# Attention heads handled four at a time instead of two at a time in a fused decoder kernel

## The reference, cut to what matters

```python
def local_attention(q, k, v):            # 16 heads of 64, windows of 64 tokens
    ...
    sim = jnp.einsum('bhwie,bhwje->bhwij', bq, bk2) * QK_SCALE
    sim = jnp.where(mask, -jnp.finfo(sim.dtype).max, sim)
    attn = jax.nn.softmax(sim, -1)
    out = jnp.einsum('bhwij,bhwje->bhwie', attn, bv2)
...
for i in range(DEPTH):                   # 6
    x = attn_layer(shift_tokens(x), Wqkv[i], q_scale[i], k_scale[i], Wo[i]) + x
    x = ffn_layer(shift_tokens(x), ln_g[i], ln_b[i], W1[i], b1[i], W2[i], b2[i]) + x
```

## Time and profile before

| | us |
|---|---|
| median of 3 runs | 3348.35 (3347.62 to 3349.45) |
| the profiled execution, its own time | 3347.67 |
| its span in the profile | 3345.9 |
| ahead of the first feed-forward block (first L831) | 260.7 |
| an ordinary slot | 62.4 |
| the longer slots at a change of layer | 67.0 to 76.4 |
| TensorE / VectorE / ScalarE / GpSimd busy | 2950.3 / 2440.5 / 2211.5 / 1464.3 |

### The profile page before, as it was taken

One profiled execution on the slowest core, in us unless ns is written; L12 is line 12 of the kernel. 1 busy time (PEld: TensorE's weight loads), 2 busy tenths in 40 slices (PEclk: granted clock), 3 DMA queues, 4 the chain that ended last, 5 costly groups with the idle time before them and its releaser, 6 DMA issues.

```text
span 3345.9 us, 83253 instructions
## 1 busy us (share of the span) xinstructions
PE 2950.3 (88%) x26408; PEld 2463.4 (74%) x26408; DVE 2440.5 (73%) x8851; ACT 2211.5 (66%) x6256; POOL 1464.3 (44%) x1052
## 2 busy tenths in 40 slices
PE   6778998888999888999988999988999988898996
PEld 5567877777777767777776777766777767777775
DVE  3477777777777777777777777777777777777773
ACT  3357667666676666767666766766676666667663
POOL 3354454334444444445443444433544543454450
PEclk9899999999999999999999999999999999999997
DMA  4210010111001111100112010012101011110000
GB/s 136 68 40 23 17 30 22 40 57 53 22 17 30 42 50 49 30 22 17 30 53 71 18 30 22 17 40 76 35 20 27 24 41 48 35 32 27 27 26 21
DMA packets 109664, 124.10 MB, mean 37 GB/s; under 512 B 11589, under 2 KB 84129, under 8 KB 109473
## 3 DMA queue, kind: packets, MB, share of 16 engines
q1 hardware_dynamic: 109472, 121.75, 12.7%
HBM read 73.50 MB, written 16.78 MB: 27 GB/s over the span
## 4 chain that ended last, share of the span: by engine, by line
PE 44%; DVE 27%; ACT 11%; issue 11%; DMA 2%; DVEq 1%; POOL 1%; SPq 0%; ACTq 0%; POOLq 0%
PE project L791 12%; PE wide L844 7%; DVE with_sin L1137 6%; PE acc L859 6%; PE score L878 5%; DVE sums_sq L1134 4%; PE acc L821 4%; DVE probs L1215 4%; DVE probs L1223 3%; PE turned L891 2%; PE mix L905 2%; DVE sums_sq L1139 2%; ACT L982 2%; ACT with_sin L949 2%; ACT probs L1019 2%
## 5 line engine op out<-in xcount | busy, mean ns | idle before, releaser
L791 PE MATMUL project<-w_qkv,xT 128*128 128x512 f32 x3456 | 953.3, 415 | 37.8 <-DVE xT L1117 33.8
L1050 POOL TENSOR_TENSOR query_scale<-sums_sq,half 128x8 f32<-128x8 f32 x192 | 412.9, 2151 | 1230.8 <-DVE sums_sq L1139 1225.8
L1019 ACT ACTIVATE probs<-probs,shift 128x128 f32<-128x128 f32 x1536 | 605.4, 396 | 430.5 <-DVE shift L1215 425.2
L791 PEld LDWEIGHTS project<-w_qkv,xT 128*128 128x128 f32 x3456 | 628.2, 194 | 172.7 <-DVE xT L1117 41.9
L1215 DVE CUSTOM_DVE_ANT_0 probs<-score,mask,query_scale 128x128 f32<-128x128 f32 x1536 | 468.7, 342 | 304.1 <-PE score L878 290.3
L844 PE MATMUL wide<-nT,w_up 128*128 128x256 f32 x3456 | 493.6, 293 | 149.2 <-ACT gates L982 87.5
L844 PEld LDWEIGHTS wide<-nT,w_up 128*128 128x128 f32 x3456 | 444.5, 194 | 201.9 <-ACT gates L982 108.9
L1053 POOL TENSOR_TENSOR inv_norm<-sums_sq,half 128x8 f32<-128x8 f32 x192 | 411.2, 2141 | 224.5 <-DVE sums_sq L1139 223.1
L1223 DVE TENSOR_SCALAR probs<-probs,inv_sums 128x128 f32<-128x128 f32 x1536 | 381.5, 291 | 0.0
L1134 DVE TENSOR_REDUCE sums_sq<-with_sin 128x8 f32<-128x512 f32 x384 | 261.8, 682 | 78.8 <-ACT with_cos L950 78.6
L1137 DVE TENSOR_TENSOR with_sin<-with_cos,tables 128x512 f32<-128x512 f32 x384 | 301.9, 786 | 13.3
(11 more groups left out here) (121 smaller groups left out, 5099.3 us busy)
## 6 DMA issues: line engine op xcount, KB each, us to landing
v_mid<-v SPq DMA_DIRECT2D x192, 128.0 KB, 2.3
staging<-in_w_qkv SPq DMA_DIRECT2D x24, 768.0 KB
y_in<-y_scratch SPq DMA_DIRECT2D x48, 256.0 KB, 2.8
res<-y_scratch SPq DMA_DIRECT2D x48, 256.0 KB, 2.7
y_scratch<-res SPq DMA_DIRECT2D x40, 256.0 KB, 2.4
staging<-in_w_up SPq DMA_DIRECT2D x12, 682.0 KB
staging<-in_w_out SPq DMA_DIRECT2D x6, 1024.0 KB
xn<-res SPq DMA_DIRECT2D x48, 112.0 KB, 2.3
```

The costliest lines, as they stand in the source:

```text
L791: last = pe.matmul(project[(x - 1) % 2][:], xT[a][:, h, t * P:(t + 1) * P], w_qkv[w][:, h, c, g, :], start=(h == 0 and (a, w) == PASSES[0] ...
L1019: last = act.activation(probs[:, t % 4, cols], probs[:, t % 4, cols], ACT.Exp, bias=shift[:, t % 2, i:i + 1], scale=-1.0, accum_out=sums[: ...
L1050: pool.tensor_tensor(query_scale[:, u // 2, g * GROUP_HEADS:(g + 1) * GROUP_HEADS], sums_sq[:, u, :], half[:, 0:GROUP_HEADS], ALU.pow).the ...
```

## The change

Heads are handled in quads. In tick 0 of every four TensorE scores four heads and mixes the quad before. VectorE masks two heads in tick 0 and two in tick 1, and scales two in tick 1 and two in tick 2; ScalarE's exponentials stand in ticks 0 and 1, ahead of its cast of `oT`. TensorE transposes two heads in tick 2 and two in tick 3. The casts of `oT` and their low parts cover four heads in one instruction, the latter one tick later; the reciprocals cover two heads. `probsT` holds four heads and `shift` four; `score` uses all of its 512 columns; `w_up` is laid out anew to make room. `SCHEDULE` is as it was. The core of the diff (names on the + side have other line numbers after the change):

```diff
-            def pair_scores(s, t, H):
+            def quad_scores(s, t, H):
...
-                for w, first in enumerate((0, 0, WINDOW, P)):
-                    for side, rows in enumerate(sides):
...
+                for k in range(QUAD_HEADS // 2):
+                    pair = t // 2 + k
+                    for w, first in enumerate((0, 0, WINDOW, P)):
+                        for side, rows in enumerate(sides):
+                            at = k * BAND + (w // 2) * P
+                            last = pe.matmul(score[side][sides[w % 2], at:at + P], qT[rows, pair, w * WINDOW:(w + 1) * WINDOW],
+                                             kT[rows, pair, first:first + P], start=True, stop=True)
+                            if w == 3:
+                                last.then_inc(scores_ready, 1)
+
+            def turn_pair(k, H):
+
+                pe.wait_ge(probs_scaled, H + 2)
+                wait(pe, probsT_copied, H)
...
-                    if t % 2 == 0 and s.head(t, 0) is not None:
-                        pair_scores(s, t, s.head(t, 0))
-                    if t % 2 == 0 and s.head(t, 4) is not None:
-                        pair_mix(s.n, (t - 4) % HEADS, s.head(t, 4), s.n * PAIRS + (t - 4) // 2)
-                    if t % 2 == 1 and s.head(t, 2) is not None:
-                        turn_pair((t - 2) % HEADS, s.head(t, 2))
+                    q = t % QUAD_HEADS
+                    if q == 0 and s.head(t, 0) is not None:
+                        quad_scores(s, t, s.head(t, 0))
+                    if q == 0 and s.head(t, 4) is not None:
+                        quad_mix(s.n, (t - 4) % HEADS, s.head(t, 4), s.n * PAIRS + (t - 4) // 2)
+                    if q == 2 and s.head(t, 2) is not None:
+                        turn_pair(0, s.head(t, 2))
+                    if q == 3 and s.head(t, 3) is not None:
+                        turn_pair(2, s.head(t, 3) + 2)
...
+                    q = t % QUAD_HEADS
+
+                    k = 2 * (q % 2)
+                    H = s.head(t, q)
+                    if H is not None and q < 2:
+                        for j in range(k, k + 2):
+                            act.wait_ge(scores_masked, H + j + 1)
+                            for i in range(TILES):
...
+                    if H is not None and q >= 2:
+                        act.wait_ge(probs_turned, H + k + 2)
+                        wait(act, mixed, H)
+                        act.copy(probsT[:, k:k + 2, :].rearrange("p a b -> p (a b)"), turned[:]).then_inc(probsT_copied, 2)
                     H = s.head(t, 4)
-                    if H is not None and t % 2 == 0:
+                    if H is not None and q == 0:
...
+                        act.copy(oT[0][:, pair:pair + 2, :], mix[:]).then_inc(out_high, 2)
...
+                    done = 2 * (q - 1)
+                    if H is not None and q in (1, 2):
+                        dve.wait_ge(exp_done, H + done + 2)
+                        dve.reciprocal(inv_sums[:, done:done + 2, :], sums[:, done:done + 2, :]).then_inc(sums_inverted, 2)
+                    if H is not None and q < 2:
...
+                        dve.wait_ge(scores_ready, H + QUAD_HEADS)
+                        wait(dve, probs_turned, H)
+                        for k in (2 * q, 2 * q + 1):
...
+                    if H is not None and q in (1, 2):
+
+                        dve.wait_ge(sums_inverted, H + done + 2)
+                        for k in (done, done + 1):
...
+                    if q == 1 and s.head(t, 5) is not None:
...
+                        dve.tensor_tensor(oT[1][:, pair:pair + 2, :], mix[:], oT[0][:, pair:pair + 2, :].bitcast(FP32),
+                                          ALU.subtract).then_inc(out_split, 2)
```

More of the change, by code:

```diff
@@ L570, in sem @@
             return ctx.enter_context(nc.semaphore(name))
-        w_qkv, w_out, w_up, w_down = W.qkv, W.out, W.up, W.down
+        w_qkv, w_out, w_up, w_down = W.qkv, W.out, W.up_flat, W.down
         params = sb("params", [P, 2 * FFN_TILES + 2 * HALVES])
@@ L862, in dense @@
                     last.then_inc(h_used, 1)
-            def pair_scores(s, t, H):
-                pair = t // 2
+            sides = [slice(HEAD_DIM * side, HEAD_DIM * side + HEAD_DIM) for side in range(2)]
+            def quad_scores(s, t, H):
                 if t % GROUP_HEADS == 0:
@@ L1213, in slot @@
-                        dve.sem_inc(passed, 1)
-                        for i, (a, b) in enumerate(((0, P), (P, BAND))):
-                            last = dve.tensor_tensor_reduce(out=probs[:, t % 4, a:b], in0=score[t % 2][:, a:b], in1=mask[:, a:b],
-                                                            scale=query_scale[:, i, t:t + 1], scalar=3e38, op0=ALU.add, op1=ALU.min,
-                                                            accum_out=shift[:, t % 2, i:i + 1])
-                        last.then_inc(scores_masked, 1)
```

95 lines of the change are left out of this document (37 added, 58 removed).

## The result

The changed kernel takes 3679.96 us (median of 4 runs, 3670.98 to 3718.72), against 3347.98 us before: a ratio of 1.102, with a 95% interval of 1.093 to 1.110. It is slower, as forecast, but by 332 us where 200 were forecast (3548), and it lies above the range of 3430 to 3640. The profiled execution is the longest of the four, 3718.72 us.

What follows compares the result with a forecast made beforehand. TensorE sets the pace but no engine is full, so list order decides its idle time. Stretches of 1.9 + 0.5 + 1.8 = 4.2 us per slot, in all 200 us, take 3347.7 to 3548; range 3430 to 3640.

Steps and rivals of the forecast that it cites:

- the clock: Rival: clock falls in ordinary slots too, two waits each costing 1.3 us more, 125 us, total 3670; chance 0.10.
- its own last part: Signs to look for: first gate's wait 2.4 us, second's 2.1, last `down` about 1, ordinary slots 66 to 67 at clock 1.00.
- The sum of the waits: Added TensorE waits over all slots: 4.2 us for each slot, half in the first, in all 200 us.
- scores of tick 8 to those of tick 12: Stretch around the gates: later `nT`, GELU and copy make it 1.8 to 1.9 us longer.
- ticks 12 to 15: Stretch up to the last `down`: VectorE's longer list in tick 13 delays it, net 0.5 us.
- ticks 0 to 8: Stretch with rotations and projections: later scales and other waits, less the lost wait for masks, net 1.8 us.
- First gate: Ticks 8 and 9, behind `nT`: starts 1.65 us later, at 6.9, of which 0.85 are wait.
- Second gate: Tick 9, behind ScalarE's GELU: 5.2 us behind the first gate instead of 4.44, 0.75 more; wait from 1.4 to about 2.1.
- Last `down`: TensorE's last `down`, behind VectorE's 2.6 us list in tick 13 and a 2.6 us chain: starts 1.0 us after TensorE is free.
- Transposes of tick 3: Transposes of the second pair's probabilities wait 1.9 us for VectorE's scales, which stand behind the later rotations.
- waits absorb one another: Rival: VectorE and ScalarE catch up while TensorE waits, half the sum stays, 100 us, total 3448; chance 0.12.
- Not slower: Rival: cover in TensorE's list suffices for all three chains, total 3300 or 3348; chance 0.07, of which 0.04 faster.

Runs made afterwards that it cites:

- Experiment 4: Kernel before the change, with one more head's exponentials on ScalarE ahead of the other work of ticks 8 and 9: 3460.72 us, ratio 1.034.
- experiment 1: Changed kernel with filler matmuls on TensorE ahead of the waits of the first gate, second gate and last `down`: 3553.46 us, ratio 1.062.
- experiment 2: Changed kernel with filler matmuls at one place only: ahead of the last `down` 3613.16 us; ahead of the two gates 3624.21 us.
- experiment 8: Kernel before with fillers at two gates: 3340.20 us; sized, in weight-loading slots only: 3332.61; those plus four ahead of tick 9's transposes: 3333.49.
- experiment 7: Changed kernel with token scaling and the cast of `nT` ahead of the exponentials in ScalarE's tick 8: 3694.84 us, ratio 1.105.
- experiment 5: Kernel of experiment 1, one filler instead of three ahead of the last `down`, VectorE's scaling of two heads omitted in ticks 1 and 13: 3486.01 us.
- experiment 6: Changed kernel with tick 3's transposes of the quad's second pair behind the first half of the output projection: 3700.15 us, ratio 1.106.

## Why the prediction was wrong, and where it was right

**The step that failed is the clock.** The forecast's sum has nothing for it, and says that ordinary slots keep a clock of 1.00; all 30 of them have a stretch at 1.2 GHz, and the clock costs 127 us. The text read the 2.91 us behind a wait of 2.22 us, priced the fall into ordinary slots at 125 us (measured: 127) and its case at 3670 (measured: 3680), and then gave it 0.10. What it set against it was that waits of 1.19 and 1.37 us leave the clock at 1.00. But by its own last part these waits become 2.4 and 2.1 us long, the length of the wait in the earlier trace rows and not of those in the earlier trace rows. The forecast checked its waits against the clock of the kernel before, not against that of its own kernel. Experiment 4 brackets the difference on the kernel before: with waits of 1.19 and 1.37 no ordinary slot has a fall, with 1.75 and 2.15 all but one of 30 have. That the price came out so near is in part luck. The text had two falls of 1.3 us in every slot. The profiled execution has two stretches in nearly every ordinary slot, of which some are free, some cost 1.5 us and some 3, on the mean 3.4 us for each of these slots, and 165 us over the profiled execution of experiment 1; the other three executions of the changed kernel are 31 to 48 us shorter. The Trainium skill, "TensorE: Matmul & The Clock Gate", Part 1, has the low level as the default that activity releases; experiments 1, 2 and 8 agree, as useless matmuls hold the clock.

**The sum of the waits was right,** 200 us forecast, 207 measured with the clock held (experiment 1), 4.2 against 4.7 for an ordinary slot. By the text's three stretches, on the mean of the ordinary slots of experiment 1 against those before: scores of tick 8 to those of tick 12, 1.9 forecast, 1.6 measured; ticks 12 to 15, 0.5 forecast, 1.2 measured; ticks 0 to 8, 1.8 forecast, 1.9 measured.

That the sum holds is partly luck too, because one gain was left out. The waits of an ordinary slot grow from 4.6 to 10.4 us where the second gate waits in full, 5.8 more, and the slot by only 4.7. The rest is TensorE's own: from the start of a quad's scores to the end of its mixes 2.09 us pass (1067.32 to 1069.41), where two pairs took twice 1.19 (1501.37 to the row below), and over four quads that is 1.2 us less. The text took 0.6 for a pair's scores and 0.6 for its mixes in either kernel.

```profile
1502.56 0.66 PE L831 MATMUL wide<-ident,xn 128*128 128x128 f32 x4
```

By terms:

- First gate: the sum had the wait grow by 0.85, which gives 2.04; the text's last part says 2.4; 2.55 measured. Its start, 1.65 later by the forecast, is 1.47 later. Shown in experiments 4 and 7 to be ScalarE's list.
- Second gate: 2.1 forecast, 2.14 where the clock held ahead of it. Shown in experiment 4.
- Transposes behind the third gate: 0.25 forecast, 0.19.
- Last `down`: 1.0 forecast, 1.76 measured. This is the one term that was clearly mis-sized. The length of VectorE's list (2.6 us forecast, 1095.54 to 1098.08 measured) and of the chain behind it (2.6 forecast, 2.5 measured) were right, and experiment 5 confirms that the list sets the wait. The list begins too early in the forecast. With the `down` 0.5 us later than before and 5.2 us of list and chain ahead of it, the list would start about 5.6 us behind the scores of tick 12 (an estimate from the text's numbers); it starts 6.5 behind them. What holds it there follows below.
- Transposes of tick 3: 1.9 forecast, 1.69 measured. The mechanism was named half: experiment 6 shows a second chain, over GpSimd, that is as late, so the late start of the rotation is the cause, and not the place of the scales.
- The fourth projection 0.35 and tick 6 0.35: 0.41 and 0.55 measured. The scores' wait for masks has gone from the list, as forecast.

What holds VectorE's list of tick 13 back stands in the rows ahead of it:

```profile
1092.66 1.58 PE L863 MATMUL acc<-w_down,hT 128*128 128x256 f32 x12
...
1094.28 0.62 ACT L1000 CAST hT<-gates 128x512 fp32r<-128x512 f32 x1 [0.47 <-PE acc L863]
...
1094.93 0.69 DVE L1198 TENSOR_TENSOR hT<-gates,hT 128x512 fp32r<-128x512 f32 x1 [1.19 <-ACT hT L1000]
```

ScalarE's cast of the second value product needs the buffer `hT`, which TensorE's first `down` still reads, and this `down` now stands behind the scores and mixes of four heads. VectorE waits 1.19 us for the cast, in every ordinary slot. The text did not follow this wait for a buffer. No run moves the `down` or gives `hT` a second buffer, so this is read from the rows and not tested.

**The rivals.** That waits absorb one another (3448) is out: with the clock held they add up, and in experiment 5 the 0.78 taken off at each of two places shortens the slot by 0.79 and 0.69. Not slower is out. The place that was to decide it, the exponentials of tick 9, works as the forecast had it: experiment 4 gives the one extra head in ticks 8 and 9 a price of 1.35 us in a slot, clock aside.

**What stays open.** What decides which gate the fall comes behind, and whether the one behind the last `down` is missing, short or long: slots of 67.1 and 71.7 us have the same list, and waits of the same length ahead of the first gate and of the last `down`. The length of a wait alone does not decide it. The 1.76 us of the last `down` are followed by a fall in 29 of the 30 ordinary slots, the 1.69 us of tick 3 in none. Open is also the cause of the scatter between executions: the one of 3718.72 us had a mean granted clock of 0.914, the one of 3670.98 us 0.922.

## What to carry to other kernels

In lists that engines work through in order, two small steps put together ahead of a longer one delay everything behind them by one step; count the delay at each wait where it ends, and look whether the engine is the last to arrive there, even if it is idle a third of the time. When a forecast lengthens TensorE's waits, compare the new lengths, not the old ones, with the waits of the trace behind which matmuls run at half speed, and expect some falls to be free, where the next wait is for another engine. Useless matmuls ahead of a wait price the clock's share in one run, and are worth keeping where such waits can't be removed.

## What the runs showed of the hardware

- The clock quantises a kernel's time. All ordinary slots differ by steps of about 1.5 us: 67.1, 68.6, 70.2 and 71.7 in the changed kernel, 63.8 and 65.3 in experiment 4. A fall ahead of a wait for another engine is free (the gate of 2.85 us in the slot of 67.1, and 12 others).
- With the clock falling often, runs of the same kernel scatter more: 3670.98 to 3718.72 us here, 3552.64 to 3556.11 with the fillers.
- VectorE slows down beside GpSimd. Among the rotations of ticks 1 to 3 one product of `with_cos` and `tables`, both in SBUF, took 1.67 us and a 128x8 operation 1.01, where 0.69 and 0.17 are usual:

```profile
1116.86 1.67 DVE L1148 TENSOR_TENSOR with_sin<-with_cos,tables 128x512 f32<-128x512 f32 x1
1118.45 1.01 DVE L1150 TENSOR_SCALAR sums_sq<-sums_sq 128x8 f32<-128x8 f32 x1
```

GpSimd's operations of 128x512 in that time:

```profile
1116.69 1.28 POOL L1067 TENSOR_TENSOR with_cos<-with_cos,with_sin 128x512 f32<-128x512 f32 x1
1118.06 1.38 POOL L1070 TENSOR_TENSOR with_cos<-with_cos,inv_norm 128x512 f32<-128x512 f32 x1
```

Of the 384 products of this line, the 293 that overlap none of GpSimd's 128x512 operations take 691 to 694 ns, and the 91 that do take 1039 to 1697; before the change 50 did. Beside GpSimd's 128x8 operations they keep their 0.69. The group's mean rose from 786 ns (L1137 before) to 924 ns, and its total from 301.9 to 354.7 us. The Trainium skill, "GPSIMD Engine Reference", section 1, lists such contention for VectorE instructions with two SBUF inputs or in a 2-port mode. The trace agrees for the product, which has two SBUF inputs; for the 128x8 operation, which has one, no run shows the mode. Whether TensorE pays for these 1.8 us was not tested.
